# Graph attention layer: two chunks of edges per transpose, and the one-hots of dst made by VectorE in place

## What is computed

```
q, k, v = h @ Wq + bq, h @ Wk + bk, h @ Wv + bv
eh      = edge_attr @ We + be
hmid    = leaky_relu(concat(q[src], k[dst], eh) @ A1 + b1)
w       = softmax over all edges of mean over heads of leaky_relu(hmid @ A2 + b2)
out     = segment_sum(w * v[dst], src)
result  = x + gamma * layernorm(h @ Wn + bn + out) + beta
```

## Time and profile before

| | |
|---|---|
| median of 3 runs | 5094.11 us (5091.33 to 5094.43) |
| the profiled execution | 5090.77 us, of which the span is 5089.0 us |
| PE, DVE, ACT, POOL busy | 4457.4, 3988.6, 2813.0, 3194.0 us |
| first and last start of a scatter | 151.7 and 4237.2 us |
| moved by DMA | 1276.12 MB in 1938630 packets, 637802 of them under 512 B |

### The profile page before, as it was taken

One profiled execution on the slowest core, in us unless ns is written; L12 is line 12 of the kernel. 1 busy time (PEld: TensorE's weight loads), 2 busy tenths in 40 slices (PEclk: granted clock), 3 DMA queues, 4 the chain that ended last, 5 costly groups with the idle time before them and its releaser, 6 DMA issues. The chain is left out here.

```text
span 5089.0 us, 137207 instructions
## 1 busy us (share of the span) xinstructions
PE 4457.4 (88%) x35287; PEld 3598.7 (71%) x35287; DVE 3988.6 (78%) x9656; ACT 2813.0 (55%) x7064; POOL 3194.0 (63%) x3381
## 2 busy tenths in 40 slices
PE   8665567888899999999999999999999986997887
PEld 3544455666688878788788878887887764776776
DVE  7655556767788888888888888888888774768998
ACT  5333333444466666666666666665666542436666
POOL 2677777777777777777777777777777772000010
PEclk9888888999999999999999999999999998999999
DMA  8888877988999988988898888988888766888887
GB/s 248 196 237 258 252 232 242 271 265 259 280 317 317 317 256 258 262 261 254 262 266 262 257 256 263 263 265 250 264 263 261 224 186 176 220 230 211 227 231 211
DMA packets 1938630, 1276.12 MB, mean 251 GB/s; under 512 B 637802, under 2 KB 1830929, under 8 KB 1938444
## 3 DMA queue, kind: packets, MB, share of 16 engines
q1 hardware_dynamic: 1768101, 831.59, 62.7%
q0 software_dynamic: 154752, 435.99, 23.1%
q10 hardware_dynamic: 15592, 6.41, 0.5%
HBM read 703.28 MB, written 570.23 MB: 250 GB/s over the span
## 5 line engine op out<-in xcount | busy, mean ns | idle before, releaser
L1266 POOL DMA_INDIRECT slots<-rows,slot_i x3224 | 3104.1, 963 | 992.4 <-issue 916.9
L1321 PE MATMUL ps_row<-win,mixed 128*128 128x256 f32 x5904 | 1530.2, 405 | 115.8 <-ACT rows L1410 109.9
L1321 PEld LDWEIGHTS ps_row<-win,mixed 128*128 128x128 f32 x5904 | 1112.0, 200 | 299.3 <-ACT rows L1410 134.7
L1410 ACT ACTIVATE rows<-ps_row 128x512 f32<-128x512 f32 x1476 | 890.3, 603 | 52.5 <-PE ps_row L1321 49.7
L1407 ACT ACTIVATE rows<-lo_all 128x8 f32 (+1 forms) x403 | 87.3, 217 | 1452.2 <-DMA slots<-rows,slot_i 1452.0
L1292 PE MATMUL ps_e<-ident,edges 128*128 128x128 f32 x3224 | 511.5, 283 | 259.6 <-ACT mixed L1399 172.8
L1292 PEld LDWEIGHTS ps_e<-ident,edges 128*128 128x128 f32 x3224 | 417.0, 147 | 425.5 <-ACT mixed L1399 180.2
L773 PE MATMUL ps_z<-onehot,q_bits 128*128 128x512 bf16 (+1 forms) x2646 | 700.5, 374 | 0.2 <-DVE onehot L856 0.2
L844 ACT ACTIVATE low<-ps_z 128x512 f32<-128x512 f32 (+1 forms) x882 | 528.2, 599 | 309.1 <-PE ps_lo L757 165.6
L866 DVE TENSOR_TENSOR mid<-low,ps_z 128x512 f32<-128x512 f32 (+1 forms) x882 | 588.6, 667 | 130.0 <-ACT low L844 104.5
L1463 ACT ACTIVATE early_v<-early_v,early_weight 128x128 f32<-128x128 f32 x1960 | 600.0, 415 | 0.0
(11 more groups left out here) (217 smaller groups left out, 5713.8 us busy)
## 6 DMA issues: line engine op xcount, KB each, us to landing
u_rows<-slots SPq DMA_DIRECT2D x880, 258.0 KB, 3.2
early_v<-slots SPq DMA_DIRECT2D x490, 258.0 KB
edges<-edge_attr_dram SPq DMA_DIRECT2D x403, 256.0 KB
q_bits<-qb_tab SPq DMA_DIRECT2D x882, 96.0 KB, 3.1
slots<-no_row SPq DMA_DIRECT2D x98, 528.0 KB
slots<-rows,slot_i POOLq DMA_INDIRECT x3224
v_own<-slots SPq DMA_DIRECT2D x198, 258.0 KB, 3.3
slots<-no_row SPq DMA_DIRECT2D x98, 396.0 KB
```

The costliest lines, as they stand in the source:

```text
L1266: pool.indirect_dma_start(slots_tab[h], bass.IndirectOffsetOnAxis(slot_i[:, u, j:j + 1], 0), rows[:, u, j, :], None).then_inc(scattered[u] ...
L1321: last = pe.matmul(bank[:, j % 2, :], mixed[:, u % 2, j, :], win[:, u, :], start=True, stop=True)
L1410: nc.scalar.activation(rows[:, u, 2 * k:2 * k + 2, 0:2 * U0].rearrange("p j (a c) -> p j a c", a=2)[:, :, :, 0:D], row_bank(s, k).rearrang ...
```

## The change

- **Two chunks per transpose.** `edges` holds only features, without gaps, so its load writes one run of 2 KB per partition. `turn` makes 4 transposes per group in place of 8: two chunks side by side, so that the even chunk's features land on partitions 0 to 63 and the odd chunk's on 64 to 127 of `ps_e`, which now turns over 2 groups. `copy_feats` copies each half of the partitions (64 x 512) into its chunks of `mixed`.
- **One-hots in place.** `one_hot` no longer writes to `edges` but straight into the other half of `mixed`'s partitions, already turned: two `tensor_scalar` on 64 partitions x 512 elements (line 1540 of the new file), whose input is `rel_rows`, the group's 1,024 relative `dst` as bytes on every partition, compared with the partition's number. It stands one group later than before (s + 1, not s + 2), and waits for the window's loads of its group and for the rows of the group two before.
- **Loads.** The window is loaded twice, into `win[DE:P, u, 0]` and `win[0:DE, u, 1]`. `rel_rows` is loaded from `rel_tab` with one DRAM row of 1 KB broadcast to 128 partitions. `rel_tab` is made at the end of the projections: four `tensor_scalar` of 128 x 1024 behind `dmin`, and one store of 512 KB. In return `dst` is no longer loaded in the edge stage and `indices` loses one operation. `win`'s first memset on POOL is twice as long, and four more copies of `We A1` are made.
- **q's split.** ACT, not SP, issues `load_q`, `store_q` and the `empty` of the first slot table, with their waits, at the start of its step.

```
-                    def turn_half(s, u, b):
...
+                    def turn(s, u):
+
+                        pe.wait_ge(edges_in[u], count(s, u, 16))
+                        if at_least(s, 2):
+                            pe.wait_ge(feats_ready, s * 2 - 2)
                         for k in range(HALF):
-                            last = pe.transpose(ps_e[:, b, k, :], edges[:, u, b * HALF + k, :], ident[:])
+                            last = pe.transpose(ps_e[:, u % 2, k, :], edges[:, u, 2 * k:2 * k + 2, :].rearrange("p j f -> p (j f)"), ident[:])
                         return last
...
                         if k == 0:
-                            pe.wait_ge(win_in[u], count(s, u, 16))
-                        if k % 2 == 0:
-                            pe.wait_ge(feats_ready, s * 2 + (k // 2 + 1))
+                            pe.wait_ge(win_in[u], count(s, u, 48))
+                            pe.wait_ge(onehot_ready, s * 2 + 2)
+                            pe.wait_ge(feats_ready, s * 2 + 2)
...
                     def one_hot(s, u):
-                        if at_least(s, UNROLL):
-                            wait_turned(dve, s - UNROLL, 1)
-                        nc.vector.tensor_tensor(edges[:, u, :, DE:P],
-                                                iota_p[:, 0:WIN].rearrange("p (a b) -> p a b", a=1).to_broadcast([P, PER, WIN]),
-                                                rel_all[:, bass.ds(s, 1), :].rearrange("p a (j o) -> p (a j) o", o=1).to_broadcast([P, PER, WIN]),
-                                                ALU.is_equal).then_inc(onehot_ready, 1)
+
+                        dve.wait_ge(win_in[u], count(s, u, 48))
+                        if at_least(s, 2):
+                            dve.wait_ge(rows_made, s * HALF - HALF)
+                        ids = rel_rows[:, u, :].rearrange("q (p k a) -> q a k p", a=2, k=HALF)
+                        for b in range(2):
+                            half = slice(DE * (1 - b), DE * (2 - b))
+                            nc.vector.tensor_scalar(pairs_of(mixed, u, b)[half], ids[half, b, :, :], part[half, 2:3], None, ALU.is_equal
+                                                    ).then_inc(onehot_ready, 1)
...
                     def copy_feats(s, u, b):
-                        wait_turned(act, s, b)
-                        nc.scalar.activation(mixed[:, u % 2, HALF * b:HALF * (b + 1), :], ps_e[:, b, :, :], ACT.Copy).then_inc(feats_ready, 1)
+                        if b == 0:
+                            wait_turned(act, s)
+                        half = slice(DE * b, DE * (b + 1))
+                        nc.scalar.activation(pairs_of(mixed, u, b)[half], ps_e[half, u % 2, :, :], ACT.Copy).then_inc(feats_ready, 1)
...
-                        sp.dma_start(win[DE:P, u, :], kv_tab[bass.ds(row, WIN), :]).then_inc(win_in[u], 16)
+                        sp.dma_start(win[DE:P, u, 0, :], kv_tab[bass.ds(row, WIN), :]).then_inc(win_in[u], 16)
+                        sp.dma_start(win[0:DE, u, 1, :], kv_tab[bass.ds(row, WIN), :]).then_inc(win_in[u], 16)
+                        sp.dma_start(rel_rows[:, u, :], rel_tab[bass.ds(s, 1), :].to_broadcast([P, GE])).then_inc(win_in[u], 16)
...
                             dve.wait_ge(span_chain, 1)
+                            for c in range(CH):
+                                nc.vector.tensor_scalar(rel[:, c, :], dgroup[:, c, :], dmin[:, c:c + 1], None, ALU.subtract
+                                                        ).then_inc(span_found, 1)
                             nc.vector.tensor_tensor(dspan[:], dmax[:], dmin[:], ALU.subtract).then_inc(span_chain, 1)
...
-                    nc.vector.tensor_scalar(base_neg, ps_w[:, 0, 0:CH * P], -1.0, None, ALU.mult).then_inc(span_chain, 1)
...
+                    sp.wait_ge(span_found, 3 * CH)
+                    sp.dma_start(rel_tab.rearrange("(c g) e -> g c e", g=P), rel[:]).then_inc(first_in, 16)
...
                     def prep_step(s, u):
+                        if split_here(s, 2):
+                            store_q(s - (PREP + 2), (u - 2) % UNROLL)
+                        if split_here(s, -2):
+                            load_q(s - (PREP - 2), (u + 2) % UNROLL)
+                        if split_here(s, 0):
+                            empty(s * 2 - 2 * PREP)
+                            empty(s * 2 - (2 * PREP - 1))
```

More of the change, by code:

```diff
@@ L129, in gnn_layer @@
     h_tab = nc.dram_tensor("h_tab", [NPAD, D], F32).ap()
+    rel_tab = nc.dram_tensor("rel_tab", [CH * P, GE], U8).ap()
     acc = [nc.dram_tensor(f"acc{r}", [ZROWS, D], F32).ap() for r in range(COPIES)]
@@ L226, in gnn_layer @@
             dgroup = tmp("dgroup", [P, CH, GE], I32)
+            rel = tmp("rel", [P, CH, GE], U8)
             dmin = tmp("dmin", [P, CH])
@@ L374, in _ @@
                                      ).then_inc(d_in, 16)
-                    for a, there in ((0, src), (1, dst)):
-                        sp.dma_start(first_ids[:, a, :, :], there[0:FIRST * GE].rearrange("(g p j) -> p g j", p=P, j=PER)).then_inc(first_in, 16)
+                    sp.dma_start(first_ids[:], src[0:FIRST * GE].rearrange("(g p j) -> p g j", p=P, j=PER)).then_inc(first_in, 16)
                     sp.wait_ge(made, N_FILLED)
@@ L887, in gnn_layer @@
             lo_all = tmp("lo_all", [P, NG, PER], U8)
-            rel_all = tmp("rel_all", [P, NG, PER], U8)
+            rel_rows = tmp("rel_rows", [P, UNROLL, GE], U8)
             bkt_all = tmp("bkt_all", [P, NG, PER], U8)
-            edges = tmp("edges", [P, UNROLL, PER, P])
+            edges = tmp("edges", [P, UNROLL, PER, DE])
             mixed = tmp("mixed", [P, 2, PER, P])
@@ L1042, in bits_of, with pairs_of @@
                 return o.q_bits[:, 2 * u:2 * u + 2, m * D:(m + 1) * D]
+            def pairs_of(tile, u, b):
+                return tile[:, u % 2, :, :].rearrange("p (k a) e -> p a k e", a=2)[:, b, :, :]
             def split_here(s, late):
@@ L1494, in _ @@
                         looped(act, UNROLL, PREP, step)
+                        for n in range(2):
+                            load_q(n, n)
                         one_by_one(PREP, PREP + UNROLL, prep_step)
-                        looped(act, PREP + UNROLL, 60, prep_step)
-                        one_by_one(60, 64, prep_step)
+                        looped(act, PREP + UNROLL, 56, prep_step)
+                        one_by_one(56, 64, prep_step)
                         one_by_one(64, START, step)
@@ L1508, in indices @@
                         if c:
-                            dve.wait_ge(index_in, 32 * c if c < NSEG - 1 else 32 * c + 32)
-                        src_i, dst_i = [first_ids[:, a, 0:n, :] if c == 0 else ids[:, c % 2, 0:n, :] for a, ids in ((0, src_c), (1, dst_c))]
-                        first = base_neg[:, g0:g1].rearrange("p (g k) -> p g k", k=1).to_broadcast([P, n, PER])
-                        nc.vector.tensor_tensor(rel_all[:, g0:g1, :], dst_i, first, ALU.add)
+                            dve.wait_ge(index_in, 16 * c if c < NSEG - 1 else 16 * c + 16)
+                        src_i = first_ids[:, 0:n, :] if c == 0 else src_c[:, c % 2, 0:n, :]
                         nc.vector.tensor_scalar(share[:, 0:n, :], src_i, 0.5 - NT / 2, 1.0 / NT, ALU.add, ALU.mult
@@ L1742, in _ @@
                         for s in range(2):
-                            one_hot(s, s)
                             bucket(s, s)
+                        one_hot(0, 0)
                         place(0, 0, True)
```

111 lines of the change are left out of this document (46 added, 65 removed).

## The result

The changed kernel takes **5101.7 us** (median of 20 runs, 5097.5 to 5105.2) against 5091.7 us (median of 20, 5089.8 to 5095.7) of the kernel before in the same comparison: a ratio of 1.002, 95% interval 1.0014 to 1.0027, so 10 us slower. The direction was right, the size was not: 51 us were forecast, over the profiled run as over the median shown. The profiled execution took 5097.5 us with a span of 5095.7; it is the shortest of its 20, and 6.8 us over the profiled one of before. The traces can explain these 6.8 us; the 10 us between the medians have no trace of their own.

The account below looks back on a forecast made before the run. The prediction took POOL's descriptor instructions to pace the edge stage. 5090.8 (profiled run) + 5 for the start + 46 for DVE and POOL excluding each other gave 5142, so 5145 us as a median; range 5096 to 5205.

Parts of the forecast that it names:

- What bounds the kernel: Edge stage: POOL's own descriptor instructions set the pace, 8 x 1.265 = 10.12 us per group.
- The 8 us that were left for other engines: Edge stage: of 4085.5 us of POOL's steps, only 8 us could be given back by another engine.
- Engines that are not the bound: Edge stage: changes to PE, ACT, SP, DMA and DVE's own length cost or give 0.
- TensorE was the bound: Rival: PE's 97% held POOL back in the edge stage; 380 us come back, 4715; chance 0.05 together with DMA.
- The start, + 5: Before the first scatter: rel operations, rel_tab store, extra load issues, memset and copies add 5 us, between 1 and 9.
- The exclusion, + 46: Edge stage: the one-hot pair on DVE locks out POOL's descriptor instructions, 46 us, ends 0 and 137; forecast chance 0.70.
- My rule: A pair starting x = 0.05 to 0.51 us into POOL's instruction costs POOL x + 0.047; 139 cases x 0.325 = 45 us.
- the second way of counting: Loss per DVE operation in six index stretches, 1.43 us over 18 operations, 0.08 each; 806 of them 64 us.
- no exclusion: Rival: the one-hot's stride-8 bytes or half partitions take no second port, POOL loses nothing; 5099; chance 0.14.
- the signs: Expected in the trace: line 1540 about 430 ns, well over a hundred descriptor instructions above 1.05 us, PE near 79%.
- the longer exclusion: Rival: one-hot byte reads take 0.69 each and lock, pair 1.42 us, costing 182 us: 5281; chance 0.07.

Follow-up runs that it names:

- pool_more: Changed kernel plus a one-column memset on POOL behind each group's eighth scatter, awaited by the next group: 5465.3 us in one run, kernel before 5101.4.
- hot_psum_5: Changed kernel with each one-hot reading the partition's number from PSUM (tensor_tensor instead of tensor_scalar): 5088.8 us in one run, kernel before 5090.6.

## Why the prediction was wrong, step by step

**What bounds the kernel: right.** POOL's chain paces the edge stage; `pool_more` shows it one to one. The 8 us that were left for other engines are no waits: in the trace of before too, no gap is over 0.32 us, and they lie in longer instructions.

**Engines that are not the bound: right.** TensorE has less to do, VectorE more, ACT issues DMAs, more bytes move; `hot_psum_5` has it all and is where the kernel before is. TensorE's relief itself was overpriced at 1.13 us per group, since transposes overlap: each lasts 283 ns, but 3224 of them make 511.5 us and not 912. This busy time fell to 243.3, 0.67 us per group, and PE stands at 85%, not near 79:

```profile
L1275 PE MATMUL ps_e<-ident,edges 128*128 128x128 f32 x1612 | 243.3, 274 | 8.1 <-DMA edges<-edge_attr_dram 8.1
```

As nobody waited for PE, this error cost the forecast nothing; "TensorE was the bound" was priced too high by it. VectorE's own price was a little low: the operations take 486 ns (median), not 427, so 1.0 us per pair.

```profile
L1540 DVE TENSOR_SCALAR mixed<-rel_rows,part x806: 477/486/712, 146.9 to 4200.7; 64x512 f32<-64x512 uint8 x162
```

**The start, + 5: wrong by 5.** The timeline of the changed kernel:

```profile
129.90 2.74 DVE L619 TENSOR_SCALAR rel<-dgroup,dmin 128x1024 uint8<-128x1024 int32 x4
132.56 0.15 DVE L621 TENSOR_TENSOR dspan<-dmax,dmin 128x4 f32<-128x4 f32 x1
132.63 1.28 DVE L552 TENSOR_TENSOR tabs<-ps_m,bias 128x512 f32<-128x512 f32 x2
...
135.47 0.51 SPq L410 DMA_DIRECT2D rel_tab<-rel  x1
...
140.02 1.31 SPq L1124 DMA_DIRECT2D edges<-edge_attr_dram  x3
...
151.74 1.31 POOL L1251 DMA_INDIRECT slots<-rows,slot_i  x1 [11.47 <-issue]
```

The four operations took 2.74 us, not 3.4, and the wait for a store that stood behind `dspan` is gone altogether. The store of `rel_tab` delays nothing: the first load of edges starts 1.4 us earlier than in the earlier trace rows. From there to the first scatter it is 11.7 instead of 10.2 us, 1.5 us more, near the 1 that I had put for the loads. The two cancel. No run was made for the start alone; this is read from the two timelines.

**The exclusion, + 46: the step that failed.** That the pair lengthens POOL's instructions was right. When it does so was wrong, and with it the size, by a factor of nearly four: 12.4 us. My rule had the pair keep POOL out if the first operation was running 0.51 us into POOL's instruction, through the second one too, and charged x + 0.047 for every x between 0.05 and 0.51. Here are the changed kernel's pairs, sorted by where the first operation starts:

```
first starts, ns       pairs   mean x   POOL lost here   POOL lost in the next
50 to 510               159      267       2.2 us          none
under 50                 16       30       none            none
510 to 760               68      641       0.2 us          none
760 to 1265             158     1031       0.1 us          11.4 us
```

The prediction counted 139 cases of the first row with 0.325 us each. There were 159, and they lost 0.014 us each. POOL then ends 0.12 us behind the first operation, which is a loss only if that ends after 0.84; it gets in through the gap of 33 ns between the two, and where the second operation starts too early it is that one that waits (up to 612 ns in this row, where 479 is usual). Nearly all of the loss comes from the last row, to which the prediction had given nothing: an operation that is still running when POOL's instruction starts, and holds back what POOL does first. Even there the order counts. Where the first operation had started about 0.1 us or more before POOL's instruction (0.098 is the nearest), POOL was lengthened; in the 31 cases where it had started less than 0.09 us before, POOL took its usual 0.96 and the second operation waited:

```profile
2413.17 1.23 DVE L1540 TENSOR_SCALAR mixed<-rel_rows,part 64x512 f32<-64x512 uint8 x2
2413.22 0.96 POOL L1251 DMA_INDIRECT slots<-rows,slot_i  x1 [0.30 <-issue]
```

Why did I read the rule wrong? In both places of the earlier trace rows the timeline of the kernel before has a DVE operation just above the rows that I looked at:

```profile
734.64 0.69 DVE L1512 TENSOR_TENSOR rel_all<-early_v,score 128x512 uint8<-128x512 int32 x1
...
170.75 0.58 DVE L1512 TENSOR_TENSOR rel_all<-early_v,score 128x416 uint8<-128x416 int32 x1
```

The instruction at 170.97, which lasts 1.19 us, looked like a pair that kept POOL out to its end. By the new rule it is the other case: the operation at line 1512 ran until 0.36 us into it, and 0.36 + 0.83 is 1.19. It has two inputs in SBUF, and I gave its loss to the `tensor_scalar` operations behind it. The one at 734.77 combines both: POOL was held back first, so that the later window, where a running operation does keep it out, lay where a third operation was. In the second way of counting, most of the loss fell likewise on instructions that line 1512 or line 1520, which has two SBUF inputs too, had held back at their start (1.6 of the 2.0 us that I now find in these stretches). Both ways leaned on the same few rows, so their agreement proved nothing. The 0.12 us of the prediction holds only in the middle of POOL's instruction; behind an operation that runs at its start it is 0.83.

The Trainium skill, page "SBUF — State Buffer", section "Who interferes with whom", says that VectorE with two SBUF inputs contends with a GpSimd instruction that reads SBUF, and that with at most one it doesn't, outside the two-port modes. POOL's descriptor instruction reads the slot numbers in `slot_i`, so the first would have named line 1512, and the traces agree with both: before the change `twos` (line 1547, two SBUF inputs) cost POOL 3.2 us in 47 instructions, and `hot_psum_5` has 806 operations with one SBUF input and none of POOL's instructions lengthened by them. The same section lets whoever comes first block the other for the whole instruction. The trace differs. By that rule a one-hot operation that starts inside POOL's instruction would wait for POOL's end; but of the 159 in the first row 141 took no more than 495 ns, while POOL's instruction went on. And where an operation runs at POOL's start, POOL ends 0.83 us behind it, not 0.96. So here the lock holds only for parts of the instruction.

**The sum** in the terms of the prediction, for the profiled runs: start 0 in place of + 5, edge stage + 10.9 in place of + 46 (the pair + 12.4, other operations - 1.5), behind the last scatter - 4.3 in place of 0.

**The range** (5096 to 5205) held the result; with "no exclusion" at 5099 it had to reach down there, so this is no merit of the mechanism. The time came nearest to that rival, but its mechanism is refuted: the exclusion is there, in 131 instructions, only small. Of the signs, line 1540 came as said (some operations up to 712 ns), while 74 descriptor instructions were above 1.05 us and not well over a hundred. One side figure of the prediction doesn't come out: for the longer exclusion the count of 139 cases gives 139 x (0.278 + 1.42 + 0.119 - 0.960) = 119 us and not 182.

## What to carry to other kernels

When one engine's fixed chain paces a stage, cost a change by what it does to that engine's instructions, and read from both sides: what was running when the instruction began, and what ran in its middle. A rule that is fitted to three or four rows needs a check on the hundreds of meetings that the trace already has with other operations (`twos` ran in every group and lengthened 47 instructions); I could have sorted those by phase before predicting. And here the compare could be had with one operand in PSUM: it was 0.17 us longer each, and in the one undisturbed run cheaper for the whole.

## What the runs showed that I had not expected

A memset of 0.12 us between two of POOL's descriptor instructions, with a wait for its end, costs the chain 0.77 us, and POOL stalled every 133 us for 1.55 us besides, which the changed kernel never does. The same program took 5.09 ms in some sets of runs and 6.7 to 6.8 in others. And half the partitions hardly shorten an operation: on ACT a copy of 64 x 512 took 585 ns, that of 128 x 512 601; on VectorE the compare with one input from PSUM has a median of 691 ns at 64 x 512 in `hot_psum_5` and at 128 x 512 in the earlier trace rows.
